# Convolution norms of tiles 4 to 15 moved from VectorE to ScalarE and GpSimd in a fused decoder block

## Chip, cores and metric

The kernel runs on one core of a Trainium2 chip. The metric is the device time of one launch in microseconds. Engines have these names in the rows: PE is TensorE (PEld its weight loads), DVE is VectorE, ACT is ScalarE, POOL is GpSimd, SP is SyncE, which only issues transfers.

## What is computed

The reference is one decoder layer on x of shape (2, 1024, 256) with a context of 77 tokens per batch. It has three sublayers, each followed by a residual sum and a layer norm. The change concerns the first, a long convolution with a norm of its own:

```python
def _L0_attn_ref(x, ..., D, ln_w, ln_b):
    K = _s4d_kernel(...)                     # (256, 1024) taps
    y = irfft(rfft(x, 2 * length) * rfft(K, 2 * length).T)[:, :length, :]
    r = x + y + x * D
    mu, var = mean(r, -1), var(r, -1)
    return (r - mu) * rsqrt(var + 1e-5) * ln_w + ln_b

x = _layernorm(x + _L0_attn_ref(x, ...))           # norms 0 and 1 of the kernel
x = _layernorm(x + _L0_xattn_ref(x, ctx, ctx, ...))   # norm 2: 16 heads of 16
x = _layernorm(x + _L0_ffn_ref(x, ...))             # norm 3: dense FFN + product-key experts
```

All is float32.

## The kernel before

The 2048 tokens stand in 16 tiles of 128 tokens by 256 features in `tok`. Two tiles (one of each batch) form a group q, from 0 to 7, so tiles 4 to 15 are the groups 2 to 7. A first part, up to some 160 us, builds the taps and does the convolution in the frequency domain. Then `conv(q)` on TensorE makes the last transform of a group, ScalarE copies it to `rconv`, and the tokens of the group go through two norms:

- `ln` (VectorE, line 1457): mean and variance of both tiles of `rconv`, into `mv[:, 0]`.
- `dev0` (GpSimd, `deviation`, line 1205): `rstd = (var + eps) ** -0.5`, two small instructions.
- `residual` (VectorE, line 1462): (r - mean) * ln_w into `gtmp`, then `gtmp * rstd + tok` into `tok`, both by scalar_tensor_tensor, tile by tile, and the statistics of the new `tok` (norm 1). ln_b was added to `tok` earlier, by GpSimd (`x_bias`).
- `dev1` (GpSimd): the same as `dev0`, and a shift, -mean * rstd: four small instructions.
- `norm1` (ScalarE): `tok = tok * rstd + shift`, one activation per tile.

After it comes the main loop, in slots, one tile of attention per slot: scores (TensorE), their maximum and difference (VectorE, `score`, two halves per tile), exp (ScalarE), transposes of the probabilities (`probs`, copied out by ScalarE in three blocks), product with the values (`attend`), its scaling by the sums (VectorE, `attend`), a transpose (`turno`), the output projection (`project`, whose sum with `tok` and statistics VectorE does), then `dev2` and `norm2`. From slot 4 on, the FFN and the experts of the four tiles before run in the same slots. Slots 0 to 3 hold attention alone; there the norms of the groups 2 to 7 stand between the attention steps.

The order is written out by numbers. `plan()` gives each step a place (a start in slots plus an entry of `PLACE`, line 56), and `order(steps, engine)` sorts them for each engine by place plus an entry of `LAG` (line 72). Each engine runs its list in order. Steps wait for each other through counting semaphores, each engine's queue stopping at a wait; `own.link` and `own.done` are waits of an engine for itself. `halve` is a GpSimd step that halves the matrix `up` of the experts (line 1222).

Of the kernel before, what the change touches and what calls it, by code (L numbers as in the profile page):

```python
# [13 lines left out]
P = 128  # L14
# [29 lines left out]
RINGP = 3  # L44
HALF = 32
# [17 lines left out]
         "ln_steps": (-0.336, -0.234, 0.162, 0.013, 0.361), "tables": (0.0,),  # L63
# [14 lines left out]
       ("act", "first"): 0.034}  # L78
# [28 lines left out]
def plan():  # L107
# [30 lines left out]
    for q in range(NQ):  # L138
        steps.append((PLACE["conv"][q], ("conv", q)))
        for k, kind in enumerate(("ln", "dev0", "residual", "dev1", "norm1")):  # L140
            steps.append((PLACE["ln"][q] + PLACE["ln_steps"][k], (kind, q)))
    steps.append((2.0, ("halve", 0)))
# [137 lines left out]
def build(nc, t):  # L280

    with ExitStack() as ctx:
# [170 lines left out]
        s_xbr = sem("x_plus_bias")  # L453
        s_x1, s_x2, s_out = sem("x1_ready"), sem("x2_ready"), sem("out_ready")
# [469 lines left out]
        def _(act):  # L924
# [108 lines left out]
            for step in order(SCHEDULE, "act"):  # L1033
# [59 lines left out]
                elif kind == "best":  # L1093
                    act.wait_ge(s_zarg, n + 1)
                    fn(zexp, zexp, ACT.Exp).then_inc(s_zexp, 1)
                    own.done(s_zexp)
                elif kind == "norm1":
                    act.wait_ge(s_rstd[1], n + 1)
                    for b in range(B):
                        normalise(1, 2 * n + b, s_x1, b == 1)  # L1100
                elif kind in ("norm2", "norm3"):
                    k = int(kind[-1])
                    act.wait_ge(s_rstd[k], n + 1)
                    normalise(k, n, s_x2 if k == 2 else s_out)
                elif kind == "exps":
                    h, m = step[2], FH * n + step[2]
                    act.wait_ge(s_best, n + 1)
                    act.wait_ge(s_sx, m + 1)
                    if m >= 2:
                        act.wait_ge(s_rfr, m - 1)  # L1110
                    fn(ebuf[m % 2], sxb[m % 2], ACT.Prelu, bias=negt[:, n % 2, h:h + 1], alpha=FAR).then_inc(s_ranked, 1)  # L1111
                    own.done(s_ranked)
                    fn(ebuf[m % 2], ebuf[m % 2], ACT.Exp, bias=above[:, n % 2, h:h + 1]).then_inc(s_e, 1)  # L1113
                    own.done(s_e)
# [3 lines left out]
        def _(pool):  # L1118
# [86 lines left out]
            def deviation(k, tl, n):  # L1205

                if k:
# [4 lines left out]
                if k:  # L1212
# [5 lines left out]
            for step in order(SCHEDULE, "pool"):  # L1218
# [22 lines left out]
                elif kind in ("dev0", "dev1"):  # L1241
                    k = int(kind[-1])
                    pool.wait_ge(s_stat[k], n + 1)
                    deviation(k, 2 * n, 2)
# [7 lines left out]
        def _(dve):  # L1252
# [202 lines left out]
            for step in order(SCHEDULE, "dve"):  # L1455
                kind, n = step[0], step[1]
                if kind == "ln":

                    dve.wait_ge(s_wact, ACT_TURN[("conv", n, "a")])
                    for b in range(B):  # L1460
                        statistics(0, 2 * n + b, rconv[:, 2 * n + b, :], b == 1)
                elif kind == "residual":
# [163 lines left out]
```

## Time and profile before

| what | us |
|---|---|
| three timed runs | 673.12, 677.3, 678.12 |
| median | 677.3 |
| profiled execution | 673.18 |
| its span, first to last instruction | 671.4 |

All rows below are of the profiled execution. The page gives each engine's busy time and share of the span. A windows table gives, for stretches in us from the span's start, the busy time of each engine (with the number of instructions), then the granted clock of TensorE as a share of full speed (1.00 is 2.4 GHz, 0.50 is 1.2 GHz) and the DMA share. The chain that ended last is followed back from the last instruction to what released it. Timeline rows are: start, duration, engine, line, operation, out<-in, shape, count, and in brackets how long the engine sat idle just before, and what ended that.

### The profile page before, as it was taken

Reading aid. Unit: us, or ns where it says so; the run is one execution under the profiler, and the core shown is the slowest. Engines: PE = TensorE matmul, PEld = TensorE weight load, DVE = VectorE, ACT = ScalarE, POOL = GpSimd, SP = SyncE. Lnnn points to the kernel's source line nnn. Section 1 sums busy time; section 2 is a strip of 40 time slices with the busy share of each in tenths; the row PEclk is TensorE's granted clock in tenths of the full one; section 3 lists DMA queues with packets and bytes.
Section 4 is the critical chain, followed back from the end, with each engine's and each line's share of the span. In section 5 each row is a group of like instructions: output and inputs, shape, how many; then the busy total and the mean of one; then the engine's idle time right before and its main releaser. Section 6 shows DMA issues by size and latency. Waiting matters only on the chain.

```text
span 671.4 us, 9604 instructions
## 1 busy us (share of the span) xinstructions
PE 582.6 (87%) x3132; PEld 380.0 (57%) x3132; DVE 493.6 (74%) x966; ACT 397.7 (59%) x554; POOL 310.9 (46%) x346
## 2 busy tenths in 40 slices
PE   5559598873868689999999999999999999898996
PEld 2244376642645545455784654777655488453585
DVE  7999936383477868987667787956879795778782
ACT  4766263320424457977736797664877783687760
POOL 0747555484613466432437262363633342753451
PEclk9769699995966689999999999999999999999999
DMA  8590323775350000000000000000000000000000
GB/s 241 202 393 9 103 73 97 178 200 77 97 223 1 0 1 0 1 0 1 1 0 9 16 2 8 1 1 0 17 8 9 0 1 1 16 9 8 0 11 22
DMA packets 19874, 34.26 MB, mean 51 GB/s; under 512 B 7280, under 2 KB 14193, under 8 KB 18353
## 3 DMA queue, kind: packets, MB, share of 16 engines
q1 hardware_dynamic: 15441, 29.46, 14.2%
q10 hardware_dynamic: 4384, 4.20, 2.1%
q8 instruction: 25, 0.41, 0.3%
q14 instruction: 24, 0.20, 0.1%
HBM read 21.94 MB, written 10.65 MB: 49 GB/s over the span
## 4 chain that ended last, share of the span: by engine, by line
PE 67%; DVE 17%; ACT 7%; issue 5%; POOL 3%; DMA 0%; DVEq 0%; ACTq 0%; POOLq 0%
PE banks L807 21%; PE banks L897 8%; PE banks L902 8%; PE banks L852 5%; PE banks L874 3%; PE banks L687 3%; PE banks L829 3%; PE banks L864 3%; PE banks L697 3%; PE banks L752 2%; PE banks L838 2%; PE banks L723 2%; ACT arena L918 2%; DVE stats L1442 2%; PE banks L889 2%
## 5 line engine op out<-in xcount | busy, mean ns | idle before, releaser
L1238 POOL TENSOR_TENSOR arena<-arena 128x1024 f32<-128x1024 f32 x64 | 126.0, 1968 | 156.2 <-ACT arena L1111 155.1
L807 PE MATMUL banks<-arena 128*128 128x512 f32 x384 | 174.3, 596 | 5.7 <-issue 3.6
L807 PEld LDWEIGHTS banks<-arena 128*128 128x128 f32 x384 | 69.8, 190 | 83.2 <-issue 77.1
L1111 ACT ACTIVATE arena<-arena 128x1024 f32<-128x1024 f32 x64 | 73.6, 1150 | 7.4 <-DVE arena L1528 3.3
L1113 ACT ACTIVATE arena<-arena 128x1024 f32<-128x1024 f32 x64 | 73.6, 1150 | 2.1
L1530 DVE SCALAR_TENSOR_TENSOR arena<-arena 128x1024 f32<-128x1024 f32 x48 | 65.1, 1357 | 1.7
L1209 POOL TENSOR_SCALAR arena<-mv 128x1 f32<-128x1 f32 (+1 forms) x40 | 14.4, 361 | 103.9 <-DVE mv L1443 102.5
L1001 ACT COPY arena<-banks 128x512 f32<-128x512 f32 (+1 forms) x64 | 34.1, 533 | 46.7 <-PE banks L799 31.1
L897 PE MATMUL banks<-arena 128*128 128x256 f32 x256 | 58.4, 381 | 2.6 <-DVE tok L1566 1.2
L902 PE MATMUL banks<-arena 128*128 128x256 f32 x256 | 57.9, 379 | 0.0
L1015 ACT ACTIVATE tok<-tok,arena,rstd 128x256 f32<-128x256 f32 x48 | 28.0, 598 | 45.0 <-POOL arena L1214 44.1
L897 PEld LDWEIGHTS banks<-arena 128*128 128x128 f32 x256 | 47.4, 190 | 10.5 <-issue 3.3
L902 PEld LDWEIGHTS banks<-arena 128*128 128x128 f32 x256 | 48.6, 190 | 6.6
L852 PEld LDWEIGHTS banks<-vbd,arena 128*128 128x128 f32 (+1 forms) x320 | 41.5, 206 | 11.0 <-ACT arena L1001 6.0
L1420 DVE TENSOR_TENSOR arena<-arena,banks 128x512 f32<-128x512 f32 (+1 forms) x36 | 23.1, 683 | 32.0 <-PE banks L697 23.5
L852 PE MATMUL banks<-vbd,arena 128*128 128x51 f32 (+2 forms) x320 | 40.8, 286 | 6.3 <-ACT arena L1001 5.9
L1547 DVE SCALAR_TENSOR_TENSOR arena<-arena 128x512 f32<-128x512 f32 x32 | 28.5, 892 | 18.4 <-ACT arena L1030 17.5
L1481 DVE TENSOR_REDUCE arena<-banks 128x8 f32<-128x616 f32 x32 | 25.6, 799 | 22.3 <-PE banks L829 21.6
L838 PEld LDWEIGHTS banks<-ident,arena 128*128 128x128 f32 (+1 forms) x160 | 21.5, 153 | 22.4 <-issue 16.2
L1211 POOL TENSOR_TENSOR rstd<-arena,cols 128x1 f32<-128x1 f32 (+1 forms) x48 | 32.2, 672 | 4.0
L1091 ACT ACTIVATE arena<-banks,pcol 128x512 f32<-128x512 f32 x32 | 22.0, 687 | 19.9 <-issue 9.9
L874 PE MATMUL banks<-wsim,arena 128*128 128x512 f32 x64 | 31.1, 608 | 2.4 <-DVE tok L1566 1.5
(181 smaller groups left out, 1072.7 us busy)
## 6 DMA issues: line engine op xcount, KB each, us to landing
scr_x<-arena SPq DMA_DIRECT2D x16, 256.0 KB, 2.6
arena<-scr_x SPq DMA_DIRECT2D x2, 2048.0 KB, 10.6
scr_z<-arena ACTq DMA_DIRECT2D x14, 256.0 KB, 3.5
tok<-in_x SPq DMA_DIRECT2D x8, 256.0 KB, 5.5
arena<-scr_z SPq DMA_DIRECT2D x4, 512.0 KB
out<-tok SPq DMA_DIRECT2D x16, 128.0 KB, 1.7
arena<-scr_z SPq DMA_DIRECT2D x2, 640.0 KB
arena<-in_imat SPq DMA_DIRECT2D x1, 1152.0 KB, 5.3
```

Source lines behind the costliest of these rows:

```text
L807: ins = mm(bk[:, :], w[:, k, P * m:P * m + P], src[:, k, :], start=(k == 0), stop=(k == KC - 1))
L838: ins = nc.tensor.transpose(bk[0:m, P * (c % 4):P * (c % 4) + P], prob[:, n % 2, P * c:P * c + m], ident[:, :])
L852: ins = mm(bank[4][:, (HD + 1) * h0:(HD + 1) * h0 + k], pT[0:m, c, :], vbd[0:m, n % B, c, 0:k], start=(c == 0), stop=(c == PCH - 1), skip_ ...
L874: ins = mm(bk[:, :], x2T[:, k, P * i:P * i + P], wsim[:, k, :], start=(k == 0), stop=(k == KC - 1))
L897: mm(bk[:, 0:D], hid[:, c, P * i:P * i + P], wd[:, c, :], start=(c == 0), stop=False)
L902: ins = mm(bk[:, 0:D], aT[:, c, :], up[:, c, :], start=False, stop=(c == EC - 1))
L1001: nc.scalar.copy(out, view(bank[2 + u % 2])).then_inc(s_tev, 1)
L1111: fn(ebuf[m % 2], sxb[m % 2], ACT.Prelu, bias=negt[:, n % 2, h:h + 1], alpha=FAR).then_inc(s_ranked, 1)
L1113: fn(ebuf[m % 2], ebuf[m % 2], ACT.Exp, bias=above[:, n % 2, h:h + 1]).then_inc(s_e, 1)
L1211: ins = tt(rstd[:, k, tl:tl + n], vare[:, 0:n], cols[:, 5:6].broadcast_to((P, n)), ALU.pow)
L1238: tt(sxb[m % 2], sim[:, n % 2, h, 0:XR].unsqueeze(2).broadcast_to((P, XR, NKEYS)), sim[:, n % 2, FH + h, :].unsqueeze(1).broadcast_to((P, ...
L1530: stt(w_, e, zinv[:, h:h + 1], w_, ALU.mult, ALU.add, accum_out=rsum[:, 0:1] if h == FH - 1 else None).then_inc(s_rfr, 1)
```

## The change

For groups 2 to 7 (`EARLY = 2`) the norm of the convolution is put together differently:

- `dev0` also makes the shift -mean * rstd, so it has four small instructions.
- A new ScalarE step `norm0` computes `rconv * rstd + shift` in place, one activation per tile.
- GpSimd's new `residual` step multiplies by ln_w and adds to `tok`, one instruction each for both tiles (128x512).
- VectorE's `residual` step waits for that sum and takes only the statistics of `tok`.

Groups 0 and 1 stay as they were. `norm0` is placed 0.1 before the group's place in `ln`; GpSimd's `residual` 0.15 before the step's own place. The orders of TensorE and of the transfers are the same as before.

```diff
+EARLY = 2
...
-         "ln_steps": (-0.336, -0.234, 0.162, 0.013, 0.361), "tables": (0.0,),
+         "ln_steps": (-0.336, -0.234, 0.162, 0.013, 0.361), "norm0": (-0.1,), "tables": (0.0,),
...
-       ("act", "first"): 0.034}
+       ("act", "first"): 0.034, ("pool", "residual"): -0.15}
...
+        if q >= EARLY:
+            steps.append((PLACE["ln"][q] + PLACE["norm0"][0], ("norm0", q)))
...
+                elif kind == "norm0":
+                    act.wait_ge(s_rstd[0], n + 1)
+                    for tl in (2 * n, 2 * n + 1):
+                        ins = fn(rconv[:, tl, :], rconv[:, tl, :], ACT.Identity, scale=rstd[:, 0, tl:tl + 1],
+                                 bias=shiftn[:, 0, tl:tl + 1])
+                    ins.then_inc(s_r0, 1)
+                    own.done(s_r0)
...
-                    deviation(k, 2 * n, 2)
+                    deviation(k, 2 * n, 2, k == 1 or n >= EARLY)
+                elif kind == "residual" and n >= EARLY:
+                    r, tiles = rconv[:, 2 * n:2 * n + 2, :], tok[:, 2 * n:2 * n + 2, :]
+                    pool.wait_ge(s_r0, n - EARLY + 1)
+                    own.link(tt(r, r, lnw.unsqueeze(1).broadcast_to((P, 2, D)), ALU.mult))
+                    tt(tiles, tiles, r, ALU.add).then_inc(s_res, 1)
+                    own.done(s_res)
...
+                elif kind == "residual" and n >= EARLY:
+                    dve.wait_ge(s_res, n - EARLY + 1)
+                    for b in range(B):
+                        statistics(1, 2 * n + b, tok[:, 2 * n + b, :], b == 1)
                 elif kind == "residual":
```

In `deviation` the condition `if k:` for the shift becomes `if shifted:`.

Three places show how the orders stand. In brackets is what an instruction waits for: `norm0_stats` are the first statistics of a group, `norm1_stats` the second ones, `norm2_stats` those of a tile's projection; `norm0_rstd` and the like are the deviations, `conv_normed` is ScalarE's new step, `x_residual` GpSimd's sum.

GpSimd in slot 1 before, from the first deviation of group 3 on:

```order
L1210 TENSOR_SCALAR arena<-mv 128x2 [waits norm0_stats,norm1_rstd]
L1211 TENSOR_TENSOR rstd<-arena,cols 128x2 [waits pool_steps]
L1209 TENSOR_SCALAR arena<-mv 128x1 [waits norm2_stats,norm0_rstd]
L1210 TENSOR_SCALAR arena<-mv 128x1
L1211 TENSOR_TENSOR rstd<-arena,cols 128x1 [waits pool_steps]
L1214 TENSOR_TENSOR arena<-arena,rstd 128x1 [waits pool_steps]
L1209 TENSOR_SCALAR arena<-mv 128x2 [waits norm1_stats,norm2_rstd]
```

And the same place now:

```order
L1220 TENSOR_SCALAR arena<-mv 128x2 [waits norm0_stats,norm1_rstd]
L1221 TENSOR_SCALAR arena<-mv 128x2
L1222 TENSOR_TENSOR rstd<-arena,cols 128x2 [waits pool_steps]
L1225 TENSOR_TENSOR arena<-arena,rstd 128x2 [waits pool_steps]
L1220 TENSOR_SCALAR arena<-mv 128x1 [waits norm2_stats,norm0_rstd]
L1221 TENSOR_SCALAR arena<-mv 128x1
L1222 TENSOR_TENSOR rstd<-arena,cols 128x1 [waits pool_steps]
L1225 TENSOR_TENSOR arena<-arena,rstd 128x1 [waits pool_steps]
L1259 TENSOR_TENSOR arena<-arena,rows 128x512 [waits conv_normed,norm2_rstd]
L1260 TENSOR_TENSOR tok<-tok,arena 128x512 [waits pool_steps]
L1220 TENSOR_SCALAR arena<-mv 128x2 [waits norm1_stats,x_residual]
```

The first deviation has two instructions more, and the sum of group 3 stands behind the third norm's deviation (128x1) of tile 0.

ScalarE in slot 1 before, from the first block of transposed probabilities to the last:

```order
L1001 COPY arena<-banks 128x512 [waits turned_mm,pv_mm,score_exp]
L1015 ACTIVATE tok<-tok,arena,rstd 128x256 [waits norm2_rstd,turned_evac]
L1001 COPY arena<-banks 128x512 [waits turned_mm,pv_mm,x2_ready]
L1063 COPY arena<-banks 128x128 [waits turned_mm,pv_mm,turned_evac]
L1065 COPY arena<-banks 80x128 [waits act_steps]
```

And now:

```order
L1005 COPY arena<-banks 128x512 [waits turned_mm,pv_mm,score_exp]
L1019 ACTIVATE tok<-tok,arena,rstd 128x256 [waits norm2_rstd,turned_evac]
L1005 COPY arena<-banks 128x512 [waits turned_mm,pv_mm,x2_ready]
L1104 ACTIVATE arena<-arena,rstd 128x256 [waits norm0_rstd,turned_evac]
L1104 ACTIVATE arena<-arena,rstd 128x256
L1067 COPY arena<-banks 128x128 [waits turned_mm,pv_mm,conv_normed]
L1069 COPY arena<-banks 80x128 [waits act_steps]
```

The pair of group 3 stands behind the third norm of tile 0 and the second block's copy, and ahead of the third block's.

GpSimd in slot 2 before, from the third norm's deviation of tile 2 to the second norms of groups 6 and 7:

```order
L1209 TENSOR_SCALAR arena<-mv 128x1 [waits norm2_stats,norm0_rstd]
L1210 TENSOR_SCALAR arena<-mv 128x1
L1211 TENSOR_TENSOR rstd<-arena,cols 128x1 [waits pool_steps]
L1214 TENSOR_TENSOR arena<-arena,rstd 128x1 [waits pool_steps]
L1209 TENSOR_SCALAR arena<-mv 128x2 [waits norm1_stats,norm2_rstd]
L1210 TENSOR_SCALAR arena<-mv 128x2
L1211 TENSOR_TENSOR rstd<-arena,cols 128x2 [waits pool_steps]
L1214 TENSOR_TENSOR arena<-arena,rstd 128x2 [waits pool_steps]
L1209 TENSOR_SCALAR arena<-mv 128x2 [waits norm1_stats,norm1_rstd]
```

And now, from the end of the same deviation on:

```order
L1225 TENSOR_TENSOR arena<-arena,rstd 128x1 [waits pool_steps]
L1259 TENSOR_TENSOR arena<-arena,rows 128x512 [waits conv_normed,norm2_rstd]
L1260 TENSOR_TENSOR tok<-tok,arena 128x512 [waits pool_steps]
L1220 TENSOR_SCALAR arena<-mv 128x2 [waits norm1_stats,x_residual]
L1221 TENSOR_SCALAR arena<-mv 128x2
L1222 TENSOR_TENSOR rstd<-arena,cols 128x2 [waits pool_steps]
L1225 TENSOR_TENSOR arena<-arena,rstd 128x2 [waits pool_steps]
L1259 TENSOR_TENSOR arena<-arena,rows 128x512 [waits conv_normed,norm1_rstd]
```

The sum of group 6 stands behind that deviation, and the sum of group 7 behind the second norm's deviation of group 6.

## Rows read from the trace of the kernel before

**Rows 1.** The page: its span and its first section, busy us by engine.

```profile
span 671.4 us, 9604 instructions
...
PE 582.6 (87%) x3132; PEld 380.0 (57%) x3132; DVE 493.6 (74%) x966; ACT 397.7 (59%) x554; POOL 310.9 (46%) x346
```

**Rows 2.** Windows table, attention slots and the part behind: stretch, its length, busy times.

```profile
186.00:199.00 13.00, 8.57 (x38) 6.93 (x38) 10.10 (x22) 3.85 (x7) 3.23 (x8) 0.65 0.57 243
199.00:212.00 13.00, 10.37 (x48) 7.14 (x49) 9.78 (x23) 4.93 (x10) 2.89 (x10) 0.63 0.00 1
212.00:225.00 13.00, 7.08 (x32) 4.36 (x30) 11.06 (x27) 3.78 (x8) 5.85 (x12) 0.76 0.00 1
225.00:238.00 13.00, 12.48 (x45) 9.02 (x46) 10.30 (x26) 7.65 (x15) 5.71 (x14) 0.65 0.00 1
238.00:262.00 24.00, 20.69 (x83) 11.46 (x82) 16.49 (x39) 16.09 (x26) 17.79 (x24) 0.93 0.00 1
262.00:671.00 409.00, 393.60 (x1629) 253.36 (x1627) 309.74 (x659) 277.83 (x370) 173.44 (x192) 1.00 0.02 6
```

**Rows 3.** Chain that ended last, 155 to 262 us: start, duration, engine and line.

```profile
206.37 0.52 DVE arena L1466
...
209.83 0.81 DVE arena L1481
210.67 0.81 DVE arena L1482
...
213.72 0.38 ACT arena L1001
...
216.32 0.44 DVE tok L1496
...
248.66 1.98 PE banks L874 x4
```

**Rows 4.** Groups by line and form on VectorE, 160 to 260 us: busy, mean ns.

```profile
L1442 DVE BATCH_NORM_STATS2 stats<-tok 128x6 f32<-128x256 f32 x20 | 8.5, 427 | 0.7
L1466 DVE SCALAR_TENSOR_TENSOR arena<-arena,mv,rows 128x256 f32<-128x256 f32 x16 | 7.8, 486 | 0.6
L1470 DVE SCALAR_TENSOR_TENSOR tok<-arena,rstd,tok 128x256 f32<-128x256 f32 x16 | 7.8, 485 | 0.6
...
L1443 DVE BATCH_NORM_AGGREGATE mv<-stats 128x2 f32<-128x6 f32 x36 | 6.6, 182 | 1.2
```

**Rows 5.** Timeline, VectorE in slot 0.

```profile
193.62 0.18 DVE L1443 BATCH_NORM_AGGREGATE mv<-stats 128x2 f32<-128x6 f32 x1
...
194.64 0.80 DVE L1481 TENSOR_REDUCE arena<-banks 128x8 f32<-128x616 f32 x1 [0.84 <-PE banks L829]
...
199.35 0.26 DVE L1487 RECIPROCAL arena<-banks 128x16 f32<-128x16 f32 x1 [1.73 <-PE banks L852]
```

**Rows 6.** Timeline, GpSimd: first and last of a four-instruction deviation, and the halving.

```profile
193.96 0.24 POOL L1209 TENSOR_SCALAR arena<-mv 128x2 f32<-128x2 f32 x1 [4.09 <-DVE mv L1443]
...
195.35 0.20 POOL L1214 TENSOR_TENSOR arena<-arena,rstd 128x2 f32<-128x2 f32 x1
...
212.75 1.90 POOL L1224 TENSOR_SCALAR arena<-arena 128x2048 f32<-128x2048 f32 x1
```

**Rows 7.** Timeline, ScalarE: second block's copy, a pair of norm 1, one norm 2.

```profile
193.28 0.59 ACT L1001 COPY arena<-banks 128x512 f32<-128x512 f32 x1 [0.27 <-PE banks L838]
...
201.69 1.09 ACT L1015 ACTIVATE tok<-tok,arena,rstd 128x256 f32<-128x256 f32 x2
...
224.23 0.60 ACT L1015 ACTIVATE tok<-tok,arena,rstd 128x256 f32<-128x256 f32 x1 [6.31 <-POOL arena L1214]
```

**Rows 8.** GpSimd by line and form (busy, mean ns); for L1202 min/median/max ns.

```profile
L1238 POOL TENSOR_TENSOR arena<-arena 128x1024 f32<-128x1024 f32 x64 | 126.0, 1968 | 156.2 <-ACT arena L1111 155.1
L1231 POOL TENSOR_TENSOR tok<-tok,rows 128x256 f32<-128x256 f32 x32 | 23.3, 727 | 2.5
...
L1202 POOL TENSOR_TENSOR tok<-tok,rows x4: 2336/2400/2780, 148.1 to 155.8; 128x1024 f32<-128x1024 f32 x4
```

More of the change, by code:

```diff
@@ L453, in build @@
         s_xbr = sem("x_plus_bias")
+        s_r0, s_res = sem("conv_normed"), sem("x_residual")
         s_x1, s_x2, s_out = sem("x1_ready"), sem("x2_ready"), sem("out_ready")
@@ L1203, in _, with deviation @@
                     own.done(s_xbr)
-            def deviation(k, tl, n):
-                if k:
+            def deviation(k, tl, n, shifted=True):
+                if shifted:
                     nc.gpsimd.tensor_scalar(shiftn[:, k, tl:tl + n], mv[:, k, tl:tl + n, 0], -1.0, None, ALU.mult)
@@ L1211, in deviation @@
                 ins = tt(rstd[:, k, tl:tl + n], vare[:, 0:n], cols[:, 5:6].broadcast_to((P, n)), ALU.pow)
-                if k:
+                if shifted:
                     own.link(ins)
```

## Prediction

> **What bounds the kernel now.** The page comes first [rows 1]. The span is 671.4 us and the TensorE is busy for 87% of it, so anything that does not hold up the TensorE costs nothing. The table by stages comes next [rows 2], since the change touches only the six groups of tiles whose convolution norm stands among the first attention slots, at 186 to 241 us. From 262 us on the TensorE is busy 393.6 of 409 us at the full granted clock (1.00, the 2.4 GHz level): that part is bound by its matmuls. From 186 to 238 us it is not. There it works 7 to 12 us of each 13, the granted clock falls to 0.63 to 0.76, and VectorE is the busiest engine or close to it (9.8 to 11.1 of 13 us in all four stretches). The chain of work that ended last says what binds there [rows 3]: it runs from VectorE's score reductions through ScalarE and the TensorE back to VectorE, and the whole group of a residual lies on it, from 206.37 us until the score reduction at 209.83 us can start. So in these 55 us a microsecond of VectorE is a microsecond of the span, and the same holds for a microsecond in which VectorE waits. At 248.66 us the first sim matmul opens the matmul-bound part. All that comes later follows it in order, so what this start is early or late, the end is early or late.
>
> **What the change removes.** Per group VectorE loses four scalar_tensor_tensor of 0.485 us each and keeps two pairs of statistics (0.43 and 0.18 us) [rows 4]. In the chain a residual took 209.83 - 206.37 = 3.46 us [rows 3]; the two pairs alone take 2 x (0.43 + 0.18) plus small gaps, 1.36 us. That is 2.1 us less per group. If nothing else changed, the five groups 3 to 7, which VectorE runs without an idle moment around them, would give 5 x 2.1 = 10.5 us. Group 2 would give nothing, since VectorE idles there anyway until the scores at 194.64 us [rows 5].
>
> **What it adds, and where.** Three pieces now stand between the first statistics and the second.
> - GpSimd's deviation grows from two small instructions to four. The same four took 193.96 to 195.55 us, 1.6 us, and began 0.16 us after the statistics ended [rows 5, 6].
> - ScalarE shifts and scales two tiles: 1.09 us, as its pairs for the second norm take [rows 7]. A handoff between engines is about 0.1 us.
> - GpSimd multiplies and adds over 128x512, a form of which this trace has no instance with these operands. The nearest rows are tok plus a row vector: 0.727 us at 256 columns, and 2.40 us (median) at 1024 [rows 8]. A straight line between them gives 1.28 us at 512; I take 1.26 us, since the shortest of the longer ones was 2.34 us. With its gap a pair takes 2.6 us. From below it is bounded by half of the 1.97 us form, 0.98 us each, and from above by half of the longest, 1.39 us [rows 8].
>
> The Trainium skill (GPSIMD Engine Reference, section 4.1, Engine selection) advises against precisely this move: two-input elementwise work belongs on VectorE and runs about twice as long on GpSimd. By its figure in section 3.1 (4497 ns for 2048 columns) an estimate for 512 columns is 1.12 us, and the sum below would be some 2 us smaller. In this trace the factor at 256 columns is 0.727 over 0.485, 1.5 times.
>
> VectorE takes its instructions in order. Its first statistics of a group now wait for GpSimd's sum, and the scores, the attention product and the projection of the running slot are queued behind that wait. I step through the six groups; "wait" is VectorE's.
>
> *Group 2.* On ScalarE the norm stands behind the second transposed block of slot 0, which ends at 193.28 + 0.59 = 193.87 us [rows 7]. So it ends at 195.0, GpSimd's pair at 197.7, the statistics at 199.15. The scores queued behind started at 194.64 us before: 4.5 us late. VectorE then idled 1.73 us before the attention product of slot 0 [rows 5], which swallows that much: **+2.8 us**.
>
> *Group 3.* Now the order binds. GpSimd's sum stands behind the deviation of the third norm of slot 0, and ScalarE's pair behind that norm's scaling and one more copy. From the end of the projection's statistics: 0.16 + 1.6 (deviation) + 0.1 + 0.6 (third norm) + 0.6 (copy) + 1.1 (pair) + 0.1 + 2.6 + 0.1 = 7.0 us. VectorE has one set of statistics to do meanwhile, 1.36 us. Wait 5.6, less 2.1 saved: **+3.5**.
>
> *Group 4.* ScalarE's pair follows the copy that ended at 213.72 + 0.37 us; the projection and its statistics end VectorE's work 1.1 us after 216.32 us [rows 3], 3.3 us behind that copy. The new route takes 1.1 + 0.1 + 2.6 + 0.2 = 4.0 us. Wait 0.7, less 2.1: **-1.4**. Here the change does what a lighter VectorE should.
>
> *Group 5.* Behind GpSimd's sum of group 4 stands the halving of the expert matrix. Before, its 1.90 us filled idle time [rows 6]. Now the second norm of group 4 waits until it ends, then come that deviation (1.6), the third norm's (1.55), ScalarE's scaling, for which ScalarE idled 6.31 us already before [rows 7], with its handoff 0.7, a copy 0.6, the pair 1.1 and the sum 2.7. With the halving (2.0) and handoffs this is 10.4 us after the sum of group 4. VectorE has three sets of statistics (3 x 1.36) and one pair of score instructions (0.81 each [rows 3]) with handoffs, 5.8 us. Wait 4.6, less 2.1: **+2.5**.
>
> *Groups 6 and 7.* Group 6's sum is queued behind the third norm's deviation, which follows the projection directly in front of it on VectorE: 0.16 + 1.6 + 2.6 + 0.1 = 4.5 us, no other work between. Group 7's sum is queued behind the second norm's deviation of group 6 in the same way: 4.5 us. Less 2.1 each: **+2.4** twice.
>
> Sum: 2.8 + 3.5 - 1.4 + 2.5 + 2.4 + 2.4 = 12.2 us; the sim matmul moves from 248.66 to about 261 us. ScalarE's 6 x 1.09 us beyond this hide in its idle time: outside the waits above it works 3.8 to 7.7 of each 13 us [rows 2]. If that cover failed at one group, 1.1 us would come on top. TensorE's instructions and the transfers do not move.
>
> The profiled execution took 673.18 us, 1.8 more than its span; the three timed runs gave 673.12, 677.3 and 678.12 us, so it is 4.1 us under their median. I put the sum on the middle of the two levels, 675.4 us: 675.4 + 12.2 = 687.6, say 687.5 us. With a GpSimd instruction of 0.98 us the six pairs are 6 x 0.56 = 3.4 us shorter, which gives +8.8; with 1.39 us, +13.8. On bases of 673.1 and 678.1 us that is 682 to 692 us, the forecast's own range.
>
> **Rivals.**
> *The route keeps up, faster.* If GpSimd and ScalarE delivered each sum before VectorE came to it, the 10.5 us would be gained: 665 us. For it speaks that VectorE's removed instructions stand on the chain [rows 3]; it decides from the point where a group's wait stays under 2.1 us. Against it stand the orders: by the steps above only group 4 is under that.
> *The later part takes the delay back, no change.* Some 675 us, if the matmul-bound part had room. Its TensorE idles 409 - 393.6 = 15.4 us in all [rows 2], and everything there is queued behind the slots that are late. I see no wait in it that ends on something else.
> *The clock makes it worse.* With longer waits the TensorE is idle more, and the granted clock, 0.93 at 238 to 262 us, might stay at the 0.65 of the stretch before [rows 2]. Its 20.7 us there would become 20.7 x 0.93 / 0.65, 9 us more; half of it on the path gives 692 us. Against it: the queries it would stretch run while VectorE waits for group 7.
>
> **How the numbers follow.** Forecast 0.77, faster rival 0.08, no change 0.07, clock 0.08. A measurement of this kernel tells about 1% (6.8 us) from no change, as its runs spread over 5 us. Slower by over 1% means above 684.1 us: the clock rival and the forecast except its lowest part, for which I take 0.10 of the 0.77, so 0.75. Within 1%: 0.10 + 0.07 = 0.17. Faster: 0.08. The range leaves out the faster rival and most of the unchanged one, and takes in the clock's price with some margin: 679 to 695 us.
>
> **What would show it.** Right: six waits of VectorE's statistics on GpSimd's sum, about 5.6, 0.7, 4.6, 4.5 and 4.5 us for groups 3 to 7; twelve 128x512 instructions on GpSimd near 1.26 us; the first sim matmul near 261 us and the stretch behind it as long as before, within 2 us; VectorE's busy time some 11.6 us (24 x 0.485) under 493.6. Wrong: a sim matmul at or before 249 us, waits under 2 us, or a matmul-bound part that becomes shorter by as much as its start is late. If the GpSimd pair is near 2 us, the mechanism holds and the sum is 9.

## The result, and the profile after

The changed kernel took 687.92 us (median of 4 runs, 686.45 to 690.05), the kernel before 677.71 us (4 runs, 673.12 to 678.31): a ratio of 1.0168, 95% interval 1.0116 to 1.0221. It is slower by more than the 1% that a measurement tells from no change, and it lies 0.4 us from the forecast of 687.5 us. The profiled execution of one later experiment (e11) was disturbed, so only that kernel's timed runs are read.

The page of the kernel after, beside [rows 1]:

```profile
span 688.2 us, 9628 instructions
...
PE 589.8 (86%) x3132; PEld 384.2 (56%) x3132; DVE 480.4 (70%) x942; ACT 404.1 (59%) x566; POOL 327.2 (48%) x370
```

VectorE works 13.2 us less, GpSimd 16.3 and ScalarE 6.4 us more: by busy time alone the change does what it says. The span is 16.8 us longer all the same. The windows table of the kernel after, beside [rows 2], tells where (stretch, length, then PE, PEld, DVE, ACT, POOL, granted clock, DMA share, GB/s):

```profile
186.00:199.00 13.00, 8.15 (x33) 4.79 (x32) 4.42 (x8) 5.60 (x10) 3.72 (x7) 0.78 0.80 339
199.00:212.00 13.00, 10.12 (x43) 7.43 (x43) 8.57 (x21) 3.48 (x6) 5.53 (x14) 0.56 0.01 1
212.00:225.00 13.00, 6.45 (x30) 4.11 (x29) 6.32 (x14) 6.79 (x13) 6.09 (x12) 0.70 0.00 0
225.00:238.00 13.00, 7.44 (x37) 6.24 (x38) 6.54 (x18) 5.20 (x10) 10.14 (x17) 0.63 0.00 1
238.00:262.00 24.00, 17.24 (x70) 11.10 (x69) 10.60 (x25) 13.20 (x24) 15.96 (x32) 0.71 0.00 1
262.00:671.00 409.00, 397.91 (x1618) 251.09 (x1617) 313.08 (x672) 286.40 (x382) 182.69 (x196) 0.99 0.02 5
```

VectorE, which worked 9.8 to 11.1 of every 13 us before, now works 4.4, 8.6, 6.3 and 6.5 in the same four stretches. What it does instead is in its timeline (start, duration, engine, line, operation, shapes, and in brackets the idle time before and what ended it). Line 1459 is the statistics, line 1260 GpSimd's sum:

```profile
200.81 0.43 DVE L1459 BATCH_NORM_STATS2 stats<-tok 128x6 f32<-128x256 f32 x1 [7.49 <-POOL tok L1260]
...
217.34 0.43 DVE L1459 BATCH_NORM_STATS2 stats<-tok 128x6 f32<-128x256 f32 x1 [5.55 <-POOL tok L1260]
...
226.95 0.43 DVE L1459 BATCH_NORM_STATS2 stats<-tok 128x6 f32<-128x256 f32 x1 [0.66 <-POOL tok L1260]
...
237.75 0.43 DVE L1459 BATCH_NORM_STATS2 stats<-tok 128x6 f32<-128x256 f32 x1 [5.09 <-POOL tok L1260]
...
248.79 0.43 DVE L1459 BATCH_NORM_STATS2 stats<-tok 128x6 f32<-128x256 f32 x1 [4.41 <-POOL tok L1260]
...
254.66 0.43 DVE L1459 BATCH_NORM_STATS2 stats<-tok 128x6 f32<-128x256 f32 x1 [4.55 <-POOL tok L1260]
```

Six waits, one per moved group, 27.8 us in all. The chain that ended last, which in [rows 3] ran through VectorE's residuals, now runs through the new route; here its first score reduction, the piece at group 5, and the first sim matmul (start, duration, engine and line):

```profile
188.66 0.81 DVE arena L1502
...
225.58 1.28 POOL tok L1260
226.94 1.91 POOL arena L1235
228.92 0.23 POOL arena L1220
...
233.51 0.20 POOL arena L1225
...
234.31 0.59 ACT arena L1104
235.03 1.27 POOL arena L1259
236.38 1.28 POOL tok L1260
237.75 0.44 DVE stats L1459
...
264.01 2.08 PE banks L878 x2
```

From GpSimd's sum of group 4 (225.58 us) the chain goes through the halving of the expert matrix (L1235, 1.91 us), three deviations one behind the other (228.92 to 233.7 us), ScalarE's new norm (L1104) and the sum of group 5 to VectorE. The halving, the new norm and the sum were not on the chain before. Two deviations one behind the other and ScalarE's third norm behind them were, in the same place; from the chain of the kernel before:

```profile
221.01 0.23 POOL arena L1209
...
223.95 0.20 POOL arena L1214
224.23 0.61 ACT tok L1015
```

So GpSimd's queue stood on the path already, for some 3 us, before any work was moved to it.

The 16.8 us of the two spans fall into three parts. The head, up to the first score reduction, is 188.66 - 185.70 = 2.96 us longer, with the same instructions (last section). The stretch from there to the first sim matmul was 248.66 - 185.70 = 62.96 us and is 264.01 - 188.66 = **75.35 us**: 12.39 more. What lies behind was 671.4 - 248.66 = 422.7 us and is 424.2: 1.4 more. The stretch is the measure of all experiments below, as it leaves the head out.

### The profile page after: what moved, and what is told of

Same layout as the page of the kernel before. It is cut to its first block, busy times and chain, and to the rows that moved or that the text cites. A ratio compares the mean times of both kernels' runs of the same rounds, so it can differ in the third digit from the quotient of the medians.

```text
span 688.2 us, 9628 instructions
## 1 busy us (share of the span) xinstructions
PE 589.8 (86%) x3132; PEld 384.2 (56%) x3132; DVE 480.4 (70%) x942; ACT 404.1 (59%) x566; POOL 327.2 (48%) x370
## 4 chain that ended last, share of the span: by engine, by line
PE 62%; DVE 20%; ACT 7%; issue 5%; POOL 5%; DMA 0%; DVEq 0%; ACTq 0%; POOLq 0%
PE banks L811 21%; PE banks L901 8%; PE banks L906 8%; PE banks L878 4%; PE banks L856 3%; PE banks L833 3%; PE banks L756 2%; PE banks L727 2%; PE banks L868 2%; PE banks L842 2%; DVE arena L1423 2%; DVE stats L1459 2%; PE banks L893 2%; PE banks L691 2%; DVE arena L1420 1%
## 5 line engine op out<-in xcount | busy, mean ns | idle before, releaser
L1220 POOL TENSOR_SCALAR arena<-mv 128x1 f32<-128x1 f32 (+1 forms) x46 | 13.9, 302 | 94.7 <-DVE mv L1460 92.9
L856 PEld LDWEIGHTS banks<-vbd,arena 128*128 128x128 f32 (+1 forms) x320 | 41.6, 206 | 12.4 <-ACT arena L1005 5.2
L1459 DVE BATCH_NORM_STATS2 stats<-tok 128x6 f32<-128x256 f32 x48 | 20.5, 427 | 29.2 <-POOL tok L1260 27.8
L833 PE MATMUL banks<-kbd,arena 64*128 64x308 f32 x128 | 28.6, 526 | 11.7 <-DVE arena L1503 11.7
L1057 ACT ACTIVATE arena<-arena 128x616 f32<-128x616 f32 x32 | 22.9, 717 | 21.0 <-DVE arena L1503 20.2
L878 PE MATMUL banks<-wsim,arena 128*128 128x512 f32 x64 | 32.9, 638 | 2.4 <-DVE tok L1587 1.5
```

What stands on the lines that cost most here:

```text
L833: ins = mm(bank[g][:, 0:GH * NKV], qT[rows_of, hh, P * i:P * i + P], kbd[rows_of, b, hh, GH * NKV * g:GH * NKV * (g + 1)], start=True, sto ...
L856: ins = mm(bank[4][:, (HD + 1) * h0:(HD + 1) * h0 + k], pT[0:m, c, :], vbd[0:m, n % B, c, 0:k], start=(c == 0), stop=(c == PCH - 1), skip_ ...
L878: ins = mm(bk[:, :], x2T[:, k, P * i:P * i + P], wsim[:, k, :], start=(k == 0), stop=(k == KC - 1))
L1459: link(V.bn_stats(stats[:, tl % 2, :], src))
```

## The experiments

The theory at the start was the prediction's: VectorE's in-order waits for the route through GpSimd and ScalarE make the whole loss. The rival: the work added to GpSimd and ScalarE makes it, wherever VectorE's statistics stand. All times are in us; "behind" is the time from the first sim matmul to the end of the span. The four columns of the stretch come from one profiled execution of each kernel, so how far the measure varies from execution to execution is not known, and differences of 1 to 2 us in it are weak by themselves. The medians are those of the undisturbed timed runs, with their number in brackets.

| kernel | first score | first sim | measure | behind | median (runs) | before on the same chip |
|---|---|---|---|---|---|---|
| before | 185.70 | 248.66 | 62.96 | 422.7 | 677.71 (4) | |
| after | 188.66 | 264.01 | 75.35 | 424.2 | 687.92 (4) | 677.71 |
| e1_late | 187.95 | 256.32 | 68.37 | 425.1 | 684.46 (4) | 674.62 |
| e2_load | 186.08 | 256.25 | 70.17 | 426.8 | 684.80 (1) | 674.62 |
| e3_one | 188.93 | 257.23 | 68.30 | 424.3 | 683.28 (1) | 674.62 |
| e4_only4 | 186.94 | 248.82 | 61.88 | 424.0 | 674.66 (1) | 674.62 |
| e5_only67 | 186.21 | 253.94 | 67.73 | 426.1 | 681.78 (1) | 673.93 |
| e6_before_late | 185.32 | 256.81 | 71.49 | 427.3 | 685.90 (1) | 673.93 |
| e7_late_norm2 | 186.36 | 252.75 | 66.39 | 423.7 | 679.81 (4) | 673.93 |
| e8_before_norm2 | 186.90 | 250.48 | 63.58 | 426.4 | 675.66 (10) | 673.93 |
| e9_tuned | 185.78 | 247.22 | 61.44 | 425.8 | 675.38 (12) | 675.61 |
| e10_before_tuned | 184.95 | 247.92 | 62.97 | 427.3 | 679.35 (10) | 675.61 |
| e11_tuned_shift | | | | | 672.62 (11) | 675.74 |
| e12_before_shift | 187.01 | 238.96 | 51.95 | 443.6 | 684.39 (6) | 675.74 |

### The sum by groups: e4, e5, e3

```diff
-EARLY = 2
+MOVED = (4,)            # e5: (6, 7)
-        if q >= EARLY:
+        if q in MOVED:
```

> Only group 4 takes the new route, all other groups that of before. By the prediction's step for this group alone: a wait of 0.7 us against 2.1 us saved, stretch 61.5 us (61 to 62). If the added work is the cost, each group adds about 2 us: 65 us.

> The changed kernel with groups 6 and 7 alone moved (tiles 12 to 15); groups 2 to 5 as before. Theory (each group costs its own wait less its own saving: groups 6 and 7 each wait 4.5 us and save 2.1 us): 62.96 + 2 x 2.4 = 67.8 us for the measure (67 to 69), and VectorE waits about 4.5 us for GpSimd at each of the two. Rival (the loss is one accumulated lateness of the whole queue, which two groups alone don't build up): 63 to 65 us.

Both came out as the sum by groups has it: 61.88 and 67.73. VectorE's waits for the sum, of e4_only4:

```profile
219.32 0.43 DVE L1459 BATCH_NORM_STATS2 stats<-tok 128x6 f32<-128x256 f32 x1 [0.67 <-POOL tok L1260]
```

and of e5_only67:

```profile
238.71 0.43 DVE L1459 BATCH_NORM_STATS2 stats<-tok 128x6 f32<-128x256 f32 x1 [4.75 <-POOL tok L1260]
...
244.59 0.43 DVE L1459 BATCH_NORM_STATS2 stats<-tok 128x6 f32<-128x256 f32 x1 [4.55 <-POOL tok L1260]
```

A group costs its own wait less what VectorE saves on it, alone as well as among the others. Lateness does not have to build up first. Group 4, whose route is nearly ready in time, gains 1.1 us.

e3_one leaves out GpSimd's multiplication by ln_w:

```diff
-                    own.link(tt(r, r, lnw.unsqueeze(1).broadcast_to((P, 2, D)), ALU.mult))
```

> As the changed kernel, but GpSimd leaves out the multiplication by the norm's weight for groups 2 to 7 (that part of the computation is left out), so its step is one instruction of 1.27 us and not two. In-order wait: each wait of VectorE is 1.3 us shorter, that of group 4 goes to nothing (0.66): 5 x 1.3 + 0.66 = 7.2 us less, stretch about 68 us (67 to 69.5). If ScalarE's pairs or a lower clock of TensorE were the cost, it would stay at 74 to 75 us.

The measure is 68.30, as the theory had it: the route is on the path with its full length. Without one of its GpSimd instructions VectorE's waits are 19.9 us in five instead of 27.8 in six, and the measure falls by 7.05 us.

### VectorE's wait covered, and the load alone: e1, e2

e1_late places the statistics of the second norm, its deviation and ScalarE's second norm half a slot later for the groups 2 to 7, so that the sum is there before VectorE comes to it.

```diff
+            late = LATE if q >= EARLY and kind in ("dev1", "norm1") else 0.0        # LATE = 0.5
-            steps.append((PLACE["ln"][q] + PLACE["ln_steps"][k], (kind, q)))
+            steps.append((PLACE["ln"][q] + PLACE["ln_steps"][k] + late, (kind, q)))
...
+        return LATE if engine == "dve" and y[0] == "residual" and y[1] >= 2 else 0.0
```

> As the changed kernel, but for groups 2 to 7 VectorE's second statistics, GpSimd's second deviation and ScalarE's second norm are placed half a slot later, so that the sums of GpSimd are ready before VectorE comes to them. The measure is the stretch from the first score reduction to the first sim matmul: 62.96 us before (185.70 to 248.66), 75.35 us changed (188.66 to 264.01). In-order wait of VectorE (my theory): its six waits, 27.8 us in all, go to under 3 us, and what is left is the 2.1 us per group that VectorE saves; the stretch is 52 to 57 us and the time about 1.2% under that of before. Rival, the added work of ScalarE and GpSimd is the cost: it is all still there, so the stretch stays at 72 us or more and the kernel slower than before.

VectorE's waits on the sum went from 27.8 us to none, but the measure fell by 7.0 us only, to 68.37: neither what the theory nor what its rival expected. The timeline of e1_late shows what stood just under the wait that was taken away (ScalarE, then TensorE):

```profile
208.83 0.60 ACT L1025 ACTIVATE tok<-tok,arena,rstd 128x256 f32<-128x256 f32 x1 [4.00 <-POOL arena L1231]
227.27 0.60 ACT L1025 ACTIVATE tok<-tok,arena,rstd 128x256 f32<-128x256 f32 x1 [6.74 <-POOL arena L1231]
...
228.54 1.95 PE L862 MATMUL banks<-vbd,arena 128*128 128x51 f32 x8 [5.93 <-ACT arena L1011]
```

ScalarE's third norm waits for its deviation, which now stands in GpSimd's queue behind sums, the halving and deviations of other groups. The copy of transposed probabilities (L1011) is queued behind it on ScalarE, and TensorE's product with the values waits for that copy, 5.93 us. The kernel before has a wait of 5.91 us at the same product (225.50 us), but there VectorE has its own work until the product is done: between 186 and 266 us it waits 1.7 us for attention products, and 12.9 us in e1_late.

e2_load leaves VectorE's norm as before and makes the new steps of ScalarE and GpSimd in their new places on a scratch buffer that nobody reads.

```diff
-                        ins = fn(rconv[:, tl, :], rconv[:, tl, :], ACT.Identity, ...
+                        ins = fn(aside[:, n % 3, tl % 2, :], rconv[:, tl, :], ACT.Identity, ...
-                    tt(tiles, tiles, r, ALU.add).then_inc(s_res, 1)
+                    tt(r, r, lnw.unsqueeze(1).broadcast_to((P, 2, D)), ALU.mult).then_inc(s_res, 1)
...
-                elif kind == "residual" and n >= EARLY:
-                    dve.wait_ge(s_res, n - EARLY + 1)
```

> VectorE does all of the kernel before, its four scalar_tensor_tensor per group included, and waits for nothing new; ScalarE's pairs and GpSimd's pairs (two multiplications by the weight) run in their new places, into a scratch ring of three, and nobody reads the result. In-order wait: the stretch from first score reduction to first sim matmul is 63 to 66 us (before 62.96), as only a copy or two stands behind a pair of 1.1 us. Added work as the cost: 73 to 75 us, as in the changed kernel.

The measure is 70.17, between both: 7.2 us from added work for which nothing waits by name. The timeline of e2_load, VectorE, GpSimd and ScalarE:

```profile
218.81 2.98 DVE L1486 SCALAR_TENSOR_TENSOR arena<-arena,mv,rows 128x256 f32<-128x256 f32 x2
...
242.38 2.11 DVE L1486 SCALAR_TENSOR_TENSOR arena<-arena,mv,rows 128x256 f32<-128x256 f32 x2
...
219.57 1.95 POOL L1238 TENSOR_SCALAR arena<-arena 128x2048 f32<-128x2048 f32 x1
...
227.56 0.60 ACT L1020 ACTIVATE tok<-tok,arena,rstd 128x256 f32<-128x256 f32 x1 [8.22 <-POOL arena L1228]
```

The third norm's wait on GpSimd, 6.31 us before [rows 7], has become 8.22. Besides, a pair of VectorE's scalar_tensor_tensor that takes 1.00 us elsewhere took 2.98 and 2.11 us while GpSimd was reading (last section). The 24 of the moved groups took 14.9 us in place of 11.6, and the 1.98 us by which the first pair is longer lie on the chain that ended last. The changed kernel has no such instructions in the groups 2 to 7, so this part of the 7.2 us is e2's own. There are then two in-order waits on GpSimd's queue, VectorE's and, a little shorter and hidden by it, ScalarE's.

### Is it the order alone? e6, e8

```diff
# e6: the kernel before, steps as late as in e1_late
+            late = LATE if q >= 2 and kind in ("dev1", "norm1") else 0.0
# e8: the kernel before, ScalarE's third norms of tiles 0 to 2 later
+        return NORM2_LATE if engine == "act" and y[0] == "norm2" and y[1] < 3 else 0.0     # 0.45
```

> The kernel before, all norms on VectorE, with the residual and second statistics of groups 2 to 7 placed half a slot later, as in e1_late: the order of e1_late without the moved work. Theory (e1_late's gain of 7.0 us over the changed kernel came from the waits that the later place covers; VectorE waits for nothing at these steps in the kernel before): the measure stays within 2.5 us of 62.96 us. Rival (half a slot later is simply the better order, waits or not): 55 to 59 us.

The measure is 71.49, far from both. The place that helps the changed kernel by 7.0 us costs the kernel before 8.5. The waits in e6_before_late between 186 and 262 us (us in total, times, longest):

```profile
POOL arena L1215 <- DVE mv L1449: 44.3, 6, 16.1
...
ACT tok L1021 <- POOL arena L1220: 21.2, 4, 6.4
```

GpSimd stops in front of the deviations of the late statistics (44.3 us), the third norm's deviation is queued behind them, and ScalarE waits 21.2 us for it, 17.4 of them before the first sim matmul; in the kernel before it was 11.0 us in the same window. The half slot is therefore no better order in itself: by this run e1_late's place also cost something, and the moved work at that place was 71.49 - 68.37 = 3.1 us better than the work left on VectorE.

> The kernel before with one thing alone: the third norm of token tiles 0 to 2 stands 0.45 of a slot later in ScalarE's order. In the kernel before ScalarE waits 6.3 us for GpSimd at tile 1 in this place (the row at 224.23 us). Theory (this wait holds the copies of the next tile's probabilities, and by them TensorE and VectorE): the measure falls from 62.96 us to 56 to 60 us and the time by 3 to 6 us. Rival (the wait is covered: VectorE's queue is as late at that point): 62 to 64 us and no difference in the time.

The measure is 63.58 and the ratio 1.0022 (0.9996 to 1.0048), as the rival had it. The wait did not go away altogether. ScalarE in e8_before_norm2:

```profile
223.88 1.09 ACT L1020 ACTIVATE tok<-tok,arena,rstd 128x256 f32<-128x256 f32 x2 [4.15 <-POOL arena L1219]
```

Of the 6.31 us [rows 7] 4.15 have moved to the next step in ScalarE's queue, the second norms of group 4, and the last copies of the probabilities wait behind it. TensorE's product was done earlier all the same (226.68 us in place of 228.29), but VectorE came to it at 229.98 us without a wait, which, less the heads' difference of 1.20 us, is the 228.79 us of the kernel before. What was taken away was covered by VectorE's own queue. An engine's long wait does not set the time merely by being long.

### Both waits moved, and a third: e7, e9, e10

> The measure is the time from the first score reduction on VectorE to the first similarity matmul on TensorE: 62.96 us before, 75.35 us after, 68.37 us when the statistics of groups 2 to 7 were placed half a slot later (the run before, e1_late). This run is e1_late with one thing more: the third norm of token tiles 0 to 2 stands 0.45 of a slot later in ScalarE's order, behind the copies of the next tile's probabilities (those copies were held by it for 4.0 and 6.7 us there, as it waited for a deviation that stands in GpSimd's queue behind other work). Theory (two in-order waits: VectorE's on the route, and, hidden just under it, ScalarE's third norm on GpSimd's queue): with both gone the measure falls well below e1_late, to 55 to 63 us, and the time comes to within 1% of the kernel before, either way. Rival (what is left is the work added to ScalarE and GpSimd itself, 1.2 us a group on the one and 2.5 us on the other, which lies on the path wherever it stands): the measure stays at 66 to 69 us.

The measure is 66.39, the rival's number, but for another reason than the rival's; the time is 1.0093 of the kernel before, within the theory's 1%. The timeline of e7_late_norm2, GpSimd's halving, ScalarE, TensorE:

```profile
221.13 1.90 POOL L1244 TENSOR_SCALAR arena<-arena 128x2048 f32<-128x2048 f32 x1
...
226.34 1.09 ACT L1113 ACTIVATE arena<-arena,rstd 128x256 f32<-128x256 f32 x2 [6.44 <-POOL arena L1234]
...
228.08 1.07 PE L865 MATMUL banks<-vbd,arena 128*128 128x34 f32 x4 [7.18 <-ACT arena L1078]
```

Now the new norm of group 5 itself (L1113) waits on ScalarE for a deviation that stands behind the halving, and the last copies of the probabilities wait behind it. It is the same kind of wait one step further on, so e9_tuned moves this place too, and the halving and GpSimd's sum with it:

```diff
-    steps.append((2.0, ("halve", 0)))
+    steps.append((0.6, ("halve", 0)))
-       ("act", "first"): 0.034, ("pool", "residual"): -0.15}
+       ("act", "first"): 0.034, ("pool", "residual"): 0.15,
+       ("act", "norm0"): 0.31}
```

> e7_late_norm2 (measure 66.39 us from the first score reduction to the first similarity matmul, where the kernel before takes 62.96 us) with what held TensorE for 7.2 us at group 5 taken away: there ScalarE's new norm of group 5 stood ahead of the last copies of tile 2's probabilities and waited 6.4 us for a deviation that stood in GpSimd's queue behind group 4's multiply and add, the halving (1.90 us) and a third norm's deviation. Three places are changed: the halving goes into GpSimd's empty time at the start (place 0.6 in the place of 2.0), ScalarE's new norms stand 0.31 of a slot later, GpSimd's multiply and add 0.30 later. Theory (what is left of the loss is again an in-order wait, now ScalarE's on GpSimd, and not the amount of work): the measure falls by 4 to 8 us, to 58 to 62.5 us, and the time is 0 to 5 us below the kernel before. Rival (every place on these queues only moves the wait to the next step, the chain VectorE, GpSimd, ScalarE, GpSimd, VectorE being longer than the stretch allows): 64.5 us or more.

The measure is 61.44, as the theory had it: the amount of work was not the limit, and 13.9 us of the stretch came back by places alone. The time is that of the kernel before, ratio 1.0008 (0.9991 to 1.0026); no gain is to be seen, as the part behind was 425.8 us, 3.1 longer than in the kernel before, whose 422.7 is the shortest of all. Why it is longer was not found. What is left in e9_tuned, ScalarE and TensorE:

```profile
245.46 1.09 ACT L1029 ACTIVATE tok<-tok,arena,rstd 128x256 f32<-128x256 f32 x2 [2.97 <-POOL arena L1235]
...
247.22 3.48 PE L888 MATMUL banks<-wsim,arena 128*128 128x512 f32 x4 [3.26 <-ACT arena L1015]
```

> The kernel before, all norms on VectorE, with the order of e9_tuned where it has the same steps: statistics of groups 2 to 7 half a slot later, third norms of tiles 0 to 2 0.45 of a slot later on ScalarE, the halving at 0.6. The late statistics alone took the measure to 71.49 us. Theory (that loss was ScalarE's third norm waiting for GpSimd behind deviations that come late with the statistics, so the later third norm gives it back; and the moved work, once its waits are covered, is worth the 2.1 us a group that VectorE saves): 62 to 67 us, and above e9_tuned by 2 to 8 us. Rival (the order and not the moved work makes the difference): within 1.5 us of e9_tuned, or below it.

The control, with VectorE doing all norms in the same order, has 62.97 in the measure, only 1.5 us above e9_tuned, at the border of the two expectations; by the timed runs, 679.35 against 675.38, it is 4.0 us above. So 24 instructions of 0.485 us less on VectorE [rows 4], 11.6 us, are worth 1.5 to 4 us once most of the waits are gone. Even that is not all their own work: in e10 three of them, from 237.72 us on, were held by GpSimd's reads (last section), 1.1 us in all.

### Out of the stretch: e11, e12

e11_tuned_shift is e9_tuned with one more edit, and e12_before_shift is the kernel before with this edit alone:

```diff
-          "ln": (-1.672, -1.4042, 0.3146, 1.2224, 1.9378, 2.3695, 3.0308, 3.1386),
+          "ln": (-1.672, -1.4042, 0.3146, 1.2224, 3.9378, 4.3695, 5.0308, 5.1386),
```

> e9_tuned (measure 61.44 us, time as before) with all steps of groups 4 to 7 (tiles 8 to 15), on every engine, two slots later in the order, most of them so behind the first similarity matmul; their tokens are turned only in slot 6 and later. Theory (the stretch before the first similarity matmul is set by VectorE, GpSimd and ScalarE waiting on each other, behind it TensorE is busy 97% of the time and the others have room): the measure falls to 50 to 57 us, TensorE's share behind it stays, and the time comes 3 to 9 us under the kernel before. Rival (what leaves the stretch is paid behind it, as the sums over keys and the experts' products wait for the same engines): the measure falls as much, the rest grows by as much, and the time is within 2 us of the kernel before or above it.

> The kernel before, all norms on VectorE, with groups 4 to 7 two slots later on every engine, as in e11_tuned_shift, and nothing else. Theory (the later place is the gain, and moving work between the engines adds little): the measure falls from 62.96 us to 51 to 58 us and the time is 3 to 8 us under the kernel before, within 2 us of e11_tuned_shift. Rival (behind the first similarity matmul VectorE is the engine that has no room for 3.46 us a group, so that there the moved work pays): at least 3 us above e11_tuned_shift.

e12 is the rival's case: 684.39 us, 1.0119 of the kernel before (1.009 to 1.0147). Its measure fell to 51.95, 11.0 us less than before, but the part behind grew by 20.9 us. The windows table of the kernel before and of e12_before_shift, 250 to 300 us:

```profile
250.00:300.00 50.00, 48.28 (x175) 25.04 (x174) 44.50 (x98) 41.61 (x58) 23.54 (x18) 1.00 0.00 1
```

```profile
250.00:300.00 50.00, 36.70 (x117) 18.58 (x115) 40.85 (x100) 34.91 (x50) 25.37 (x29) 0.83 0.00 1
```

and the timeline of e12_before_shift, VectorE's residual and the expert's step behind it, and TensorE's products held by them:

```profile
282.57 1.32 DVE L1466 SCALAR_TENSOR_TENSOR arena<-arena,mv,rows 128x256 f32<-128x256 f32 x2
...
287.99 0.69 DVE L1541 SCALAR_TENSOR_TENSOR arena<-arena,banks 128x512 f32<-128x512 f32 x1
...
288.73 2.08 PE L807 MATMUL banks<-arena 128*128 128x512 f32 x2 [4.16 <-DVE arena L1541]
```

TensorE, which the later part is bound by, is busy 11.6 us less there, and at a granted clock of 0.83 in place of 1.00. At 288.73 us it has waited 4.16 us for an expert's step of VectorE (L1541), and in front of that step stand a whole residual (L1466, from 282.57 us) and a score. VectorE was busy 44.5 of these 50 us before and has little room. The changed kernel in the same place (e11) took 672.62 us, 0.9963 of the kernel before (0.994 to 0.9985) and 11.8 us less than e12. By the medians that is 3.1 us under the kernel before, by the ratio 2.5, at the lower edge of its theory's 3 to 9; the measure and the part behind, of which both its expectations speak, are not known. It is the one version that is faster than the kernel before, by 0.4%. That it is so because VectorE is relieved where it is short is argued from e12 and not shown: e11 has e9's other places besides, which e12 has not, and the kernel before with both was not run.

## Why the prediction was right

- **The six waits.** Predicted 5.6, 0.7, 4.6, 4.5, 4.5 us for the groups 3 to 7; measured 5.55, 0.66, 5.09, 4.41, 4.55. For group 2 the text put the end of GpSimd's sum at 197.7 us; it came at 200.7, and the head had started the stretch 2.96 us late.
- **The sum by groups.** VectorE's four attention products of tiles 0 to 3 started at 199.35, 211.50, 228.79 and 242.65 us before and at 205.19, 220.37, 239.10 and 257.69 after. Less the 2.96 us of the head they are 2.9, 5.9, 7.4 and 12.1 us late. The steps gave 2.8 (group 2), 6.3 (with 3), 7.4 (with 4 and 5) and 12.2. e4 and e5 confirm single terms: -1.1 for -1.4, and +4.8 for +4.8. The first sim matmul came at 264.01 us and not near 261; the 3 us between are the head's.
- **GpSimd's instruction.** Estimated by a straight line between two shapes at 1.26 us; the twelve took 1.26 to 1.27 (below). The Trainium skill's figure (GPSIMD Engine Reference, section 3.1), scaled to 512 columns, gave an estimate of 1.12 us; the measurement decides for the line between this trace's own rows.
- **The part behind.** 1.4 us longer, within the 2 us that were named. It gives nothing back.
- **The clock rival.** Its condition came true in part, its price did not. The granted clock at 238 to 262 us was 0.71 and not 0.93, but the last attention product was 12.1 us late and the first sim matmul 12.4, so that the lower clock can have cost some 0.3 us on the way between them. The first sim matmuls ran at 2.08 us for two, where the kernel before took 1.98 for four [rows 3]; that is of the size of the 1.4 us behind.
- **VectorE's busy time** fell by 13.2 us, not 11.6. The 24 instructions account for 11.6; a single tensor_scalar over 128x1024 near 600 us, which took 2.29 us before and 0.75 after, for 1.5.
- **The base.** The profiled executions differ by 16.9 us (690.05 and 673.18), the medians by 10.2, the stretch by 12.4: the head, which took 184.95 to 188.93 us in the runs of the table, is mixed into the first two. The base of 675.4 us was 2.3 under the measured 677.71, and the sum of 12.2 was 2.0 over the medians' difference; that the two nearly cancel is luck. The interval of the ratio, 7.9 to 15.0 us, does not tell 10.2 from 12.2.

GpSimd's two new instructions in the kernel after, by line and form (busy us, mean ns | idle before):

```profile
L1260 POOL TENSOR_TENSOR tok<-tok,arena 128x512 f32<-128x512 f32 x6 | 7.6, 1268 | 0.5
L1259 POOL TENSOR_TENSOR arena<-arena,rows 128x512 f32<-128x512 f32 x6 | 7.6, 1267 | 10.9 <-ACT arena L1104 10.7
```

Two steps of the text were wrong without showing in its number. The first is the faster rival's price: "If GpSimd and ScalarE delivered each sum before VectorE came to it, the 10.5 us would be gained: 665 us." In e1 each sum was there, and the stretch was 5.4 us longer than before. In e9, with only 3.5 us of such waits left, it was 1.5 us shorter. The reading behind it, that a microsecond of VectorE is a microsecond of the span here, holds for a wait that is put in, and not for work that is taken out: below VectorE's queue the next chain, GpSimd to ScalarE to TensorE, is nearly as long. The chain of the kernel before showed it: from 221.01 to 225.50 us it runs through GpSimd and ScalarE's third norm, which the text left out when it read the chain as going from VectorE through ScalarE and TensorE back to VectorE. The second is "ScalarE's 6 x 1.09 us beyond this hide in its idle time". In the changed kernel no such cost is to be seen beside VectorE's waits. With these not there the added load of both engines cost 7.2 us (e2), part of it VectorE stopped by GpSimd's reads; what ScalarE's pairs cost by themselves was not tried.

## What to carry to other kernels

When work is moved from a busy engine to idle ones, write out the whole route of handoffs, put each new step into the in-order queue it will stand in, and compare the moment the result is there with the moment its consumer comes to it; the busy times say nothing of this. If it comes too late, move the consumer and whatever the helpers' queues hold up (here copies for TensorE behind a norm), one wait after another, and have a control with the same order and the work not moved. The gain, if any, is to be looked for where the relieved engine is short and holds the bound one, and not simply where it is busiest; for this last part e11 and e12 are a hint and no proof.

## What the runs showed of the hardware that was not expected

A head that nothing was changed in took 2.96 us longer. Windows table of the kernel before, in the head, and the timeline row of TensorE there:

```profile
115.80:119.40 3.60, 3.55 (x79) 2.83 (x79) 0.00 (x0) 1.01 (x2) 0.34 (x1) 1.00 0.50 122
```

```profile
115.85 1.96 PE L723 MATMUL banks<-arena 128*32 128x128 f32 x64 [2.86 <-issue]
```

and the same of the kernel after:

```profile
115.80:119.40 3.60, 3.50 (x64) 3.22 (x64) 0.00 (x0) 0.00 (x0) 0.00 (x0) 0.50 0.59 142
```

```profile
115.90 3.64 PE L727 MATMUL banks<-arena 128*32 128x128 f32 x64 [2.87 <-issue]
```

The granted clock of this stretch is 1.00 (2.4 GHz) in the one and 0.50 (1.2 GHz) in the other, after the same idle time of 2.9 us and at the same point of the span; the same 64 matmuls take 1.96 and 3.64 us. They are 1.7 of the head's 2.96 us. The change need not have a part in it: e8_before_norm2, whose head is that of the kernel before, was granted 0.56 in this window. Nor is it all: e1_late was granted 1.00 there, and its head was 187.95 us long. It may be part of what separates the 673 and 678 us of the kernel before, which was not tried.

VectorE's scalar_tensor_tensor over 128x256 and GpSimd's longer instructions get in each other's way. The first pair of e2_load, from the chain that ended last, and GpSimd's timeline beside it:

```profile
218.81 0.96 DVE arena L1486
...
219.80 2.00 DVE arena L1486
```

```profile
218.21 1.27 POOL L1263 TENSOR_TENSOR arena<-arena,rows 128x512 f32<-128x512 f32 x1
```

Each takes 0.485 us when nothing is in its way. The first ended at 219.77 us, 0.29 after GpSimd's multiplication; the second at 221.80, 0.28 after GpSimd's tensor_scalar (219.57 to 221.52). So it was with all ten of the norms' instructions that were held for longer, five in e2, three in e10 and two in e12: wherever in GpSimd's instruction they began, they ended 0.27 to 0.29 us after it. Beside a deviation's instructions (128x2, up to 0.93 us) they kept their 0.48 to 0.51 us. The other way round, the four of e2's GpSimd instructions over 128x512 that began during one of them took 1.33 to 1.54 us in place of 1.27. In the kernel before, the halving ran beside statistics and a score reduction, which kept their 0.43 and 0.80 us. The Trainium skill (SBUF — State Buffer, Who interferes with whom) says that a VectorE instruction with two SBUF inputs contends with a GpSimd instruction that reads SBUF, and that the port pair which the two share is an exclusive lock. The ten cases agree with that.
